# Masked attention with a layer norm on one core: parts of q and k by way of DRAM instead of SBUF to SBUF

## What is computed

```python
h = jnp.maximum(_layernorm(x, axis=-1), 0.0)
q, k, v = (h @ W + b).reshape(b, n, H, HD)        # three weights, three biases
scores = einsum('bqhd,bkhd->bhqk', q, k) / sqrt(HD)
scores = scores + (1.0 - adj)[None, None, :, :] * -1000000000.0
attn = softmax(scores, axis=-1)
out = einsum('bhqk,bkhd->bqhd', attn, v).reshape(b, n, d)
return x + out @ Wo + bo
```

## Time and profile before

| | us |
|---|---|
| median of 3 runs | 1124.28 (1122.65 to 1124.87) |
| the profiled execution | 1119.4 |
| its span, first to last instruction | 1117.6 |
| PE busy | 1096.1 (98% of the span) |
| ACT busy | 997.8 (89%) |
| DVE busy | 958.5 (86%) |
| POOL busy | 315.4 (28%) |
| queue of SP's and ACT's transfers, share of 16 DMA engines | 31.6% |

### The profile page before, as it was taken

The page is one execution under the profiler, slowest core; times in us unless marked ns, Lnnn a source line. Parts: engine busy times, 40 slices in busy tenths (PEclk is TensorE's granted clock), DMA queues, the critical chain, the costliest instruction groups (busy, mean ns, idle before and its releaser), DMA issues.

```text
span 1117.6 us, 28309 instructions
## 1 busy us (share of the span) xinstructions
PE 1096.1 (98%) x10672; PEld 886.7 (79%) x10672; DVE 958.5 (86%) x1796; ACT 997.8 (89%) x1835; POOL 315.4 (28%) x508
## 2 busy tenths in 40 slices
PE   8799999999999999999999999999999999999997
PEld 6677887888878888887887887888877888878775
DVE  5698988988989888998989988998988988988885
ACT  3699999998989998999999999999999999999985
POOL 6364212232214222242212412124112242112122
PEclk9899999999999999999999999999999999999999
DMA  7842352424424243332424335242352424424111
GB/s 202 253 109 50 88 147 64 105 61 111 135 72 104 64 126 101 86 102 69 130 77 116 76 81 142 68 118 75 82 141 73 103 68 101 106 65 105 51 29 49
DMA packets 88374, 109.08 MB, mean 98 GB/s; under 512 B 24752, under 2 KB 50480, under 8 KB 88240
## 3 DMA queue, kind: packets, MB, share of 16 engines
q1 hardware_dynamic: 77040, 95.89, 31.6%
q0 software_dynamic: 11008, 11.13, 5.1%
q10 hardware_dynamic: 192, 0.26, 0.1%
HBM read 30.54 MB, written 9.44 MB: 36 GB/s over the span
## 4 chain that ended last, share of the span: by engine, by line
issue 51%; DMA 30%; POOL 15%; SPq 1%; PE 1%; DVE 0%; POOLq 0%; ACT 0%; ACTq 0%; DVEq 0%
DMA inv_rows<-inv_turned 15%; DMA inv_t<-inv_rows 14%; POOL inv_t L446 10%; POOL xn L414 3%; POOL ln_t L399 1%; POOL mask L453 1%; SPq L298 1%; PE ps_scores L752 0%; POOL ln_neg_mean L396 0%; DMA q_stack<-q_lo 0%; PE ps_heads L782 0%; PE ps_side L800 0%; POOL ln_var L397 0%; POOL ln_t L403 0%; POOL ln_t L401 0%
## 5 line engine op out<-in xcount | busy, mean ns | idle before, releaser
L567 DVE CUSTOM_DVE_ANT_0 rows<-ps_scores,mask 128x1024 f32<-128x1024 f32 x512 | 615.7, 1217 | 36.4 <-PE ps_scores L733 31.1
L478 ACT ACTIVATE rows<-rows,row_min 128x1024 f32<-128x1024 f32 x512 | 589.5, 1158 | 3.6 <-DVE row_min L567 3.6
L766 PE MATMUL ps_turn<-ident_r,rows_raw 128*128 128x128 f32 x4096 | 465.6, 258 | 11.6 <-ACT turned_a L483 10.6
L766 PEld LDWEIGHTS ps_turn<-ident_r,rows_raw 128*128 128x128 f32 x4096 | 400.4, 141 | 87.0 <-ACT rows L478 29.0
L483 ACT ACTIVATE turned_a<-ps_turn 128x512 f32<-128x512 f32 x512 | 307.7, 601 | 87.1 <-PE ps_turn L766 87.0
L733 PE MATMUL ps_scores<-k_stack,q_stack 128*128 128x512 f32 x1016 | 328.7, 423 | 0.9 <-DVE row_min L567 0.9
L574 DVE COPY turned_b<-ps_turn 128x512 f32<-128x512 f32 x312 | 215.0, 689 | 85.9 <-PE ps_turn L766 80.7
L440 POOL DMA_DIRECT2D inv_rows<-inv_turned x64 | 46.6, 727 | 622.0 <-DVE inv_turned L608 616.6
L446 POOL DMA_DIRECT2D inv_t<-inv_rows x256 | 136.0, 538 | 149.1 <-DMA inv_rows<-inv_turned 144.8
L733 PEld LDWEIGHTS ps_scores<-k_stack,q_stack 128*128 128x128 f32 x1016 | 159.5, 188 | 16.9 <-DVE row_min L567 6.2
L817 PE MATMUL ps_heads<-turned_a,v 128*32 128x256 f32 x2048 | 123.8, 382 | 0.3 <-ACT turned_a L483 0.3
(11 more groups left out here) (84 smaller groups left out, 588.8 us busy)
## 6 DMA issues: line engine op xcount, KB each, us to landing
q_stack<-q_hi SPq DMA_DIRECT2D x248, 64.0 KB, 2.0
q_stack<-q_lo SPq DMA_DIRECT2D x248, 64.0 KB, 2.0
k_stack<-k_hi SPq DMA_DIRECT2D x242, 64.0 KB, 2.0
k_stack<-k_lo SPq DMA_DIRECT2D x242, 64.0 KB, 2.0
res<-in_x SPq DMA_DIRECT2D x32, 256.0 KB, 2.8
inv_t<-inv_rows POOLq DMA_DIRECT2D x256, 32.0 KB, 2.3
out<-res SPq DMA_DIRECT2D x32, 256.0 KB, 2.8
xn<-in_x SPq DMA_DIRECT2D x30, 256.0 KB, 3.2
```

Of the source, the lines that this page charges most:

```text
L478: nc.scalar.activation(rows[:, k, :], rows[:, k, :], ACT.Exp, bias=row_min[:, k:k + 1], scale=-1.0, accum_out=row_sum[:, u % 2, j:j + 1]). ...
L567: nc.vector.tensor_tensor_reduce(out=rows[:, k, :], in0=ps_scores[n % 2][:], in1=mask[:, qt, :], scale=1.0, scalar=START_MIN, op0=ALU.add, ...
L766: tr = nc.tensor.transpose(ps_turn[half][:, k, :].bitcast(F32R), rows_raw[:, n % RING, kt * P:(kt + 1) * P], ident_r[:])
```

## The change

The four steps of each phase no longer copy from SBUF to SBUF. `bounce_step` stores the high and the low part whole (128 partitions times 512 elements, 256 KB each) to a DRAM tensor `parts_out`, waits on SP until both have landed, and loads them back in four transfers, one for each group of 32 partitions of the stack, with all four heads in one transfer (256 KB each). The semaphores follow: one for q and one for k that counts the stores (`bounced`), and one for each of q and k and phase that counts the loads (`stacked`). ACT waits for the stores before it writes `hi` again; PE waits before row 0 of a phase for all loads of that phase. The four loads of x in step 2 stand behind the four transfers back. Before the first phase everything stays as it was, with `half_stacked` in place of `stacked["q"][0]`.

```diff
--- before.py
+++ after.py
@@ -173,6 +173,8 @@
         inv_turned = sb("inv_turned", [P, SQUARE])
         inv_rows = nc.dram_tensor("inv_rows", (SQUARE, P), F32, kind="Internal").ap()
         inv_t = sb("inv_t", [P, UNIT_TILES, P])
+
+        parts_out = nc.dram_tensor("parts_out", (QK_STEPS, 2, P, BANK), F32, kind="Internal").ap()
         stats = sb("stats", [P, TILES, 6])
         mean_var = sb("mean_var", [P, TILES, 2])
         ln = {n: sb(f"ln_{n}", [P, TILES]) for n in ("neg_mean", "var", "power", "rstd", "t0", "t1", "t2")}
@@ -201,7 +203,9 @@
         x_start_in = [sem(f"x_start_in{i}") for i in range(2)]
         x_in = sem("x_in")
         res_in = [sem(f"res_in{i}") for i in range(2)]
-        stacked = {n: [[sem(f"{n}_stacked{g}_{h}") for h in range(PARTS)] for g in range(PHASES)] for n in "qk"}
+        bounced = {n: sem(f"{n}_bounced") for n in "qk"}
+        stacked = {n: [sem(f"{n}_stacked{g}") for g in range(PHASES)] for n in "qk"}
+        half_stacked = [sem(f"half_stacked{h}") for h in range(PARTS)]
         start_stacked = [sem(f"start_stacked{h}") for h in range(PARTS)]
         pool_stacked = [sem(f"pool_stacked{h}") for h in range(PARTS)]
         out_stored = sem("out_stored")
@@ -279,13 +283,13 @@
                     for i in range(ROWS):
                         slot(b, g, i, b == 0 and g == 0, b == BATCH - 1)
 
-        def stack_count(n, g, h, fills, steps_more=0):
-
-
-            count = (fills * CHUNKS + steps_more) * STEP_DMAS
-            if g == 0:
-                count -= STEP_DMAS if n == "q" else CHUNKS * STEP_DMAS
-            return count * 16
+        def stack_count(g, fills):
+
+            return (fills - (1 if g == 0 else 0)) * CHUNKS * PARTS * 16
+
+        def bounce_count(b, g, s):
+
+            return (b * PHASES + g) * CHUNKS * 32 + s // 2 * 32
 
         def parts_of(n, q_hi, k_hi, q_lo, k_lo):
             return (q_hi, q_lo, q_hi, q_lo) if n == "q" else (k_hi, k_hi, k_lo, k_lo)
@@ -320,6 +324,23 @@
 
                     sp.wait_ge(out_stored, (b * UNITS + (u + 1)) * 16)
                     load_res(nb, nu)
+
+            def bounce_step(b, g, s):
+
+                n, ng = "qk"[s % 2], 1 - g
+                cols = slice(s // 2 * BANK, (s // 2 + 1) * BANK)
+                stack = {"q": q_stack, "k": k_stack}[n][ng]
+                sp.dma_start(parts_out[s, 0], hi[s % 2][:].bitcast(F32)).then_inc(bounced[n], 16)
+                sp.dma_start(parts_out[s, 1], lo[s % 2][:].bitcast(F32)).then_inc(bounced[n], 16)
+                sp.wait_ge(bounced[n], bounce_count(b, g, s) + 32)
+                for r, part in enumerate(parts_of(n, 0, 0, 1, 1)):
+                    sp.dma_start(stack[r * HEAD_DIM:(r + 1) * HEAD_DIM, :, cols].bitcast(F32),
+                                 parts_out[s, part].rearrange("(h d) n -> d h n", d=HEAD_DIM)
+                                 ).then_inc(stacked[n][ng], 16)
+                    if g == 1 and s == 2 and b + 2 < BATCH:
+
+                        sp.wait_ge(ht_turned, (b + 2) * HT_STEPS)
+                        load_x(b + 2, r)
 
             def load_mask(part, first, end):
                 sp.dma_start(mask[:, first:end, :], adj_v[:, first:end, :]).then_inc(mask_in[part], 16)
@@ -353,7 +374,7 @@
             sp.wait_ge(scores_done, PARTS)
             load_mask(2, MASKS_EARLY, MASKS_LATE)
             sp.wait_ge(lo_done, START_QK.index(2) + 1)
-            stack_step(sp, 0, 2, stacked["q"][0])
+            stack_step(sp, 0, 2, half_stacked)
             load_mask(3, MASKS_LATE, TILES)
             for piece in range(X_PIECES):
                 load_x(1, piece)
@@ -368,12 +389,7 @@
                     for kind, s, _ in steps(g, b == 0, b == BATCH - 1):
                         if kind == "qk":
                             sp.wait_ge(lo_done, qk_step(nb, ng, s) + 1)
-                            for h in range(PARTS):
-                                stack_step(sp, ng, s, stacked["qk"[s % 2]][ng], range(h, h + 1))
-                                if g == 1 and s == 2 and b + 2 < BATCH:
-
-                                    sp.wait_ge(ht_turned, (b + 2) * HT_STEPS)
-                                    load_x(b + 2, h)
+                            bounce_step(b, g, s)
                         elif kind == "o":
                             store(*((b - 1, s) if g == 0 else (b, s)))
             store(BATCH - 1, UNITS - 1)
@@ -496,12 +512,11 @@
             def next_high_part(b, g, s):
                 n, (nb, ng) = "qk"[s % 2], next_phase(b, g)
 
-                for h in range(PARTS):
-                    if s < 2:
-                        if stack_count(n, g, h, b + 1):
-                            act.wait_ge(stacked[n][g][h], stack_count(n, g, h, b + 1))
-                    else:
-                        act.wait_ge(stacked[n][ng][h], stack_count(n, ng, h, nb, 1))
+                if bounce_count(b, g, s):
+                    act.wait_ge(bounced[n], bounce_count(b, g, s))
+                elif s == 0:
+                    for h in range(PARTS):
+                        act.wait_ge(half_stacked[h], STEP_DMAS * 16)
                 high_part(qk_step(nb, ng, s) + 1, ng, s, hi[s % 2][:])
 
             def copy_ht(b, s, bank=ps_heads[:]):
@@ -722,10 +737,10 @@
                     pe.wait_ge(pool_stacked[h], by_pool * STEP_DMAS * 16)
                     pe.wait_ge(start_stacked[h], (3 - by_pool) * STEP_DMAS * 16)
                 elif n < ROWS and i % (ROWS // CHUNKS) < PARTS:
-                    pe.wait_ge(stacked["q"][g][h], stack_count("q", g, h, fills))
-                elif i < PARTS:
-                    pe.wait_ge(stacked["q"][g][h], stack_count("q", g, h, fills))
-                    pe.wait_ge(stacked["k"][g][h], stack_count("k", g, h, fills))
+                    pe.wait_ge(half_stacked[h], STEP_DMAS * 16)
+                elif i == 0 and n:
+                    pe.wait_ge(stacked["q"][g], stack_count(g, fills))
+                    pe.wait_ge(stacked["k"][g], stack_count(g, fills))
                 if n >= 2:
 
                     pe.wait_ge(masked, n - 1)
```

## The result

The changed kernel takes 1142.99 us (median of 4 runs, 1139.24 to 1147.19) against 1123.76 us (4 runs, 1122.65 to 1124.87): 1.0178 times as long, with a 95% interval of 1.0159 to 1.0198. That is 19.2 us more; the forecast said 9 us more, at 1133.3.

A forecast was written before the change was run, and what follows sets the result against it. The prediction took PE's own work as the bound. A 0.6 us stall at each of 15 boundaries adds 9 us, with other terms at zero, on the runs' median 1124.28 us: 1133.3 us, range 1122.5 to 1144.

The forecast's parts named there:

- SP has 38 us per phase less to do: On SP, 16 issues of 0.63 us become 6 per step; worth nothing, since no engine waits for SP's time.
- The change decides at the deadline: Before row 0, the whole last step must have landed 9.45 us after the low part, at 15 boundaries.
- Step 1 of the chain: On SP in a phase's last step: first store issued 0.03 us after the low part, second at 0.62.
- Step 2: In a phase's last step, both stores landed 3.4 us after the low part, using a median 2.8 us per store.
- rival A: At the boundaries, loads back are in time, landing after 8.45 us, and nothing changes: 1124.3 us; chance 0.24.
- Steps 3 and 4: The four loads back in the last step: 1.95 us fixed plus 4.6 us for the bytes at 230 GB/s.
- sign for rival A: In the loads back, a landing before 9.4 us or rates over 300 GB/s would point to rival A.
- Step 6: On SP in the last step, some issues run longer, adding 0.1 us on average to the chain.
- The sum, 0.6 us for each boundary: At each of 15 phase boundaries PE stands 0.6 us waiting for the loads back, 9 us in all.
- Waits on ACT and PE: ACT's waits for two stores instead of copies, and PE's 45 dropped stack waits, were each valued at 0.
- More bytes: Each step moves 1.57 MB instead of 1.05; value 0, with POOL's `inv_t` covered by at least 0.9 us.
- rival B: At each boundary, stores take 4.0 us and loads run at 213 GB/s; PE waits 2.0 us: 1154 us; chance 0.08.

The follow-up runs named there:

- experiment 2: The changed kernel with the loads back in two halves, a semaphore for each half, awaited before row 0 and row 2: 1119.22 us, ratio 0.9974.
- 7: The changed kernel with the last step of each phase done by sixteen copies with semaphores by head, the other three through DRAM: 1118.91 us, ratio 0.9971.
- 8: The changed kernel with loads back in two halves, a semaphore each, and the high part stored as soon as it is ready: 1120.88 us, ratio 0.9984.
- experiment 1: The kernel before, its sixteen copies kept, with PE waiting for all stacks of a phase before row 0: 1191.77 us, ratio 1.061.
- Experiment 4: The changed kernel without POOL's round trips for the inverted sums, inv_t filled with ones: 1133.53 us, ratio 1.0086.
- experiment 5: The changed kernel with each load back filling one head's 128 partitions instead of 32 partitions of four heads: 1124.2 us, ratio 1.0022.
- 11: The kernel before, unchanged and profiled again: 1122.17 us.
- 12: The changed kernel, without further edits, profiled again: 1144.99 us.
- experiment 3: The changed kernel with two DRAM buffers in turn, loads back reading the phase before without waiting for the stores: 1180.38 us, ratio 1.0503.
- 6: The changed kernel with the high part stored when ACT has written it, before the low part is ready: 1141.88 us, ratio 1.0177.

## Why the prediction was off by half

Its steps in order:

- *PE is the bound, and a phase lasts as long as PE's own work*: right. Experiments 2, 7 and 8 have the phases of before with other transfers.
- *SP has 38 us per phase less to do*: 25 by the forecast's own numbers (4 steps of 10 issues of 0.63 us). It enters no sum.
- *The change decides at the deadline, 9.45 us after the low part, 15 times*: right; experiment 1 alone puts 47.9 us on it, 2 and 7 take it away.
- *Step 1 of the chain* (second store issued at 0.62): 0.41 at 13 of 15 boundaries, since the issues were 0.38 us apart here and not 0.6. The rows had it: the 256 KB store at 507.29 took 0.39 us, so the 0.63 "of either size" in the text on rival A is too wide as well.
- *Step 2, both stores landed at 3.4 us*: **this is the step that failed.** The loads began after 3.4 to 5.7 us, 4.35 on average. The second store took 3.6 us (median) and up to 5.3, where the view of the output's stores had a median of 2.8 and a longest of 4.0. The rows warned: POOL's four transfers stand at that very time, and I let them count for 0.3 us. A store of the same form shows the difference in the changed kernel itself, by the medians: 2.3 us in step 0, away from POOL, 3.6 in step 3. 15 times 0.95 are 14 us of waits by themselves. Experiment 4 puts about half of the loss on POOL's transfers; the rest goes with packets of the queue `instruction`, which is seen in the traces but not tested.
- *Steps 3 and 4, the loads in 6.55 us*: right, 6.5 measured, and experiment 5 supports the reason that was given, the 32 partitions. The Trainium skill's rule of the ports ("SBUF — State Buffer", "Door 1: The DMA port swizzle") says that 32 partitions reach half of the ports. These traces agree with it in direction, not in size: in the slices that are 9 tenths busy, 250 GB/s on average into 32 partitions (the Trainium skill has 218) and 352 into 128. Rival A, with a landing at 8.45 us, is out for the changed kernel: no last load landed before 9.95. The forecast's sign for rival A, rates over 300 GB/s, was badly chosen, since single slices have 306 to 415 here without it.
- *Step 6, slow issues, 0.1 us*: right in kind (501.58 took 1.60 us), small.
- *The sum, 0.6 us for each boundary*: 1.39 in one profile of the changed kernel, 1.25 in the other. With the measured store the chain would have given 10.9 and a wait of 1.45, so 22 us.
- *PE's clock*: not in the sum. Three stretches at half the clock cost 5 us in the profile.
- *Waits on ACT and PE, SP's shorter list: nothing*: right as far as seen. *The start, as before*: not quite, the first boundary comes 1.6 us earlier (experiments 11 and 12). *More bytes: nothing, with 0.9 us as the least cover*: right for the changed kernel, but its cover was nearly used up (a median margin of 0.3 us at the worst place, the first unit of a phase), and experiment 3 used it up.

The measured time was inside the range (1122.5 to 1144), about half way from the forecast to rival B, and that it was inside is in part luck: the range priced stalls of up to 1.3 us (its text calls that half of 2.0, which is 1.0) and no clock, and in the profiles two terms it left out pull against each other, the clock upward and the start downward. Rival B had the mechanism, late stores, and took them for an exception. They are the rule: none of the 15 stores took less than 3.0 us. POOL's transfers, its reason for them, are about half of it.

## What to carry to other kernels

When many small transfers become a few large ones behind one semaphore, look for the consumer that took them one by one: its first use now waits for the last landing, and with an engine that has no gaps the whole difference is paid each time round. Keep the large transfers if you like, but split the semaphore (and the transfers' order) along the order of use; here that alone turned 19 us of loss into none (experiment 2). When you price a transfer, take its duration from the rows of the moment in which it will run, beside the same neighbours, and not from the median of a quiet place.

## What the runs showed of the hardware that I had not expected

- A stall of 2 to 3 us on a PE that is otherwise busy was often followed by 3.4 or 6.8 us at half the clock (0.51 in the stretch from 443.0); each 3.4 us in which PE works costs 1.7 us. In experiment 1 eleven such stretches make up much of the 20 us beyond the waits.
- Taking away a wait on SP made the kernel 37 us slower (1180.4 against 1143.0), by letting a burst of loads run ahead of another engine's small transfers and beside them.
- A store can wait for its last few packets: two of 256 KB had moved nearly all of their bytes within 1.6 us, and the last packets took another 1.5 us, with one 16 KB packet of the queue `instruction` beside them. In six profiles of kernels with these stores (the changed one twice and experiments 2, 4, 5 and 6) the last step's second stores with such a packet are slower by 0.7 to 1.1 us (medians).
- The issue of a 256 KB store to `parts_out` took SP 0.34 or 0.43 us and that of a load from it 0.43 (medians), less than the 0.59 of a 64 KB copy from SBUF to SBUF. It doesn't go by size or direction alone: in the kernel before, the 256 KB loads took 0.38 us for `res` and 0.58 for `xn`.
